# Two attention layers per image on one core: a loop of one pass with fixed score parts, a new order of a few steps, and x copied on chip

## What is computed

```
# layer 0
theta, phi = W_theta x + b_theta, W_phi x + b_phi        # 64 channels each
f   = softmax(theta^T phi / 8)                           # 1024 x 1024 per image
x1  = x + W_fuse (x f^T) + b_fuse
# layer 1
h   = group_norm(x1, 32 groups) * gn_w + gn_b
q, k, v = W_q h + b_q, W_k h + b_k, W_v h + b_v          # 128 channels
a   = softmax(q^T k / sqrt(128))                         # 1024 x 1024 per image
y   = x1 + W_p (v a^T) + b_p
```

## Time and profile before

| what | us |
|---|---|
| runs, median of 3 (lowest, highest) | 2093.81 (2093.53, 2098.11) |
| profiled execution, its own time | 2101.46 |
| span of its instructions | 2099.7 |
| PE / DVE / ACT / POOL busy in the span | 1800.1 / 1626.3 / 1522.8 / 1549.4 |
| share of the DMA engines' time used by the kernel's queue | 73.8% |
| HBM read / written | 67.64 MB / 17.04 MB |

### The profile page before, as it was taken

One profiled execution on the slowest core, in us unless ns is written; L12 is line 12 of the kernel. 1 busy time (PEld: TensorE's weight loads), 2 busy tenths in 40 slices (PEclk: granted clock), 3 DMA queues, 4 the chain that ended last, 5 costly groups with the idle time before them and its releaser, 6 DMA issues.

```text
span 2099.7 us, 32489 instructions
## 1 busy us (share of the span) xinstructions
PE 1800.1 (86%) x8388; PEld 1417.1 (67%) x8388; DVE 1626.3 (77%) x1706; ACT 1522.8 (73%) x2249; POOL 1549.4 (74%) x1605
## 2 busy tenths in 40 slices
PE   5788888888888888888888888888888888888886
PEld 4567676666676667667666766666776667677765
DVE  5687887787888688777877887887788788878864
ACT  5577777777777677677767776776777677777754
POOL 3577777777777777777767777777777677787764
PEclk8899999999999999999999999999999999999999
DMA  5578777777777777777777777787777677777774
GB/s 116 101 145 159 142 155 149 154 140 151 149 153 157 135 148 155 149 144 146 145 146 149 149 162 142 139 157 149 145 150 148 138 146 156 157 151 153 146 127 90
DMA packets 864787, 304.16 MB, mean 145 GB/s; under 512 B 822816, under 2 KB 823712, under 8 KB 864672
## 3 DMA queue, kind: packets, MB, share of 16 engines
q1 hardware_dynamic: 864672, 302.86, 73.8%
HBM read 67.64 MB, written 17.04 MB: 40 GB/s over the span
## 4 chain that ended last, share of the span: by engine, by line
PE 34%; issue 22%; ACT 17%; DVE 16%; POOL 4%; SPq 3%; DMA 2%; DVEq 1%; ACTq 0%; POOLq 0%
PE o_ps L365 11%; PE s_ps L365 9%; ACT s_ps L553 5%; PE s_ps L400 5%; PE m_ps L365 4%; DVE x L668 3%; ACT pair L576 3%; SPq L288 3%; PE m_ps L452 3%; DVE pair L636 2%; ACT et L564 2%; DMA pair_t<-pair 2%; DVE x L680 2%; DVE neg_max L619 2%; ACT e L553 2%
## 5 line engine op out<-in xcount | busy, mean ns | idle before, releaser
L744 POOL TENSOR_SCALAR et<-pair_t 128x2048 fp32r<-128x2048 f16 x384 | 747.5, 1950 | 168.4 <-DMA pair_t<-pair 165.4
L365 PE MATMUL o_ps<-et,v_hi 128*128 128x512 f32 x2048 | 755.9, 411 | 16.8 <-DVE y_sb L668 11.2
L619 DVE TENSOR_REDUCE neg_max<-s_ps 128x1 f32<-128x1024 f32 x512 | 622.0, 1215 | 114.7 <-PE s_ps L365 109.1
L636 DVE SCALAR_TENSOR_TENSOR pair<-s_ps,pair 128x1024 f16<-128x1024 f32 x384 | 467.5, 1218 | 28.8 <-ACT pair L576 28.4
L365 PEld LDWEIGHTS o_ps<-et,v_hi 128*128 128x128 f32 x2048 | 392.3, 192 | 107.4 <-issue 22.5
L553 ACT ACTIVATE s_ps<-s_ps,neg_max 128x1024 f32<-128x1024 f32 x384 | 418.1, 1089 | 22.5 <-DVE neg_max L619 16.3
L576 ACT ACTIVATE pair<-s_ps 128x1024 f16<-128x1024 f32 x384 | 392.9, 1023 | 20.9
L365 PE MATMUL o_ps<-et,v_lo 128*128 128x512 f32 x1024 | 407.5, 398 | 0.0
L630 DVE SCALAR_TENSOR_TENSOR et<-s_ps,et 128x1024 fp32r<-128x1024 f32 x128 | 156.8, 1225 | 262.8 <-ACT et L564 262.8
L365 PE MATMUL s_ps<-phi,theta 128*128 128x512 f32 x1024 | 289.7, 407 | 18.8 <-issue 13.5
L808 POOL TENSOR_TENSOR stage<-stage 128x256 f32<-128x256 f32 x256 | 188.2, 735 | 113.0 <-ACT stage L513 102.2
(11 more groups left out here) (88 smaller groups left out, 2484.7 us busy)
## 6 DMA issues: line engine op xcount, KB each, us to landing
rden_row<-rden_dram SPq DMA_DIRECT2D x128, 256.0 KB, 4.3
xs<-in_x SPq DMA_DIRECT2D x32, 512.0 KB, 4.7
phi<-phi SPq DMA_DIRECT2D x64, 256.0 KB, 4.2
xr<-in_x SPq DMA_DIRECT2D x32, 512.0 KB, 5.3
out_y<-y_sb SPq DMA_DIRECT2D x64, 256.0 KB, 2.5
pair_t<-pair SPq DMA_TRANSPOSE x384, 4.4
rden_dram<-rden SPq DMA_DIRECT2D x128, 2.0 KB, 1.6
w_f<-in_w_fuse_t SPq DMA_DIRECT2D x1, 64.0 KB, 2.6
```

The lines of the kernel that those rows point to most:

```text
L365: mm = pe.matmul(out, lhs_t, rhs, start=start and n == 0, stop=stop and n == len(terms) - 1)
L619: nc.vector.tensor_reduce(neg_max[:, t % 4:t % 4 + 1], s_ps[:, ring(it, t), :], AX.X, ALU.max, negate=True).then_inc(s_max, 1)
L636: nc.vector.scalar_tensor_tensor(out=pair[:, r, 1, :], in0=s_ps[:, r, :], scalar=E_SCALE, in1=pair[:, r, 0, :], op0=ALU.mult, op1=ALU.subt ...
L744: return nc.gpsimd.tensor_scalar(*args)
```

## The change

The loop has one pass per round: passes 2 to 30 are looped (29 rounds), and 31 to 33 are written out. The part of `s_ps` is fixed by the slot (`PART`); the `pair` and `pair_t` buffers go by the tile's place in its group. PE does the unit ahead of the transposes. DVE's residual of the first half moves from slot 11 to 12, its statistics to 13; the second half's stay in slot 15, and all of them now come after `reciprocals`. The reciprocals are written to DRAM turned over (4 rows of 128), so that the row is in the order of the output's columns. `xr` is no longer loaded: ACT copies it from `xs` in slot 3, and `xs` is loaded in slot 4, after that copy.

```diff
-RING = 3
-TURNED = (3,)
+TURNED = 3
+PART = (0, 1, 2, 0, 1, 2, 0, 1, 2, 0, 1, 2, 0, 1, 0, 2)
+PARTS = 3
+PAIRS = 3
...
-XS_SLOT = 1
-XR_SLOT = 6
+XR_SLOT = 3
+XS_SLOT = 4
...
+    def xr_at(g):
+        i, s = divmod(g, SLOTS)
+        return int(s == XR_SLOT and 0 <= i < NB)
...
+    def part(s):
+        return PART[s % SLOTS]
+
+    def part_before(i, s):
+
+        g = SLOTS * i + s
+        return next((p for p in range(g - 1, -1, -1) if tile_at(p) and part(p) == part(g)), None)
+
+    def until_part_before(kind, it, s):
+
+        return value(lambda i: count(kind, 0, (part_before(i, s) or 0) + 1), it)
...
-    LOOPED = (NB - 3 - 2) // RING * RING
...
-        with eng.Fori(0, LOOPED // RING) as j:
-            for n in range(RING):
-                body(It(j * RING + (2 + n), 2 + n, j))
-        for i in range(2 + LOOPED, NB + 2):
+        with eng.Fori(0, NB - 3) as j:
+            body(It(j + 2, 2, j))
+        for i in range(NB - 1, NB + 2):
             body(It(i, i, 0))
...
-        rden_dram = nc.dram_tensor("rden_dram", (2, P, GROUP), F32).ap()
+        rden_dram = nc.dram_tensor("rden_dram", (2, GROUP, P), F32).ap()
...
-                sp.wait_ge(s_et, before(free_of(crossed_at), it, t + 1))
+                sp.wait_ge(s_et, before(crossed_at, it, t - GROUP + 1))
...
-                sp.dma_start(rden_dram[g], rden[:, g, :]).then_inc(s_rden_dram[g], 16)
+                sp.dma_start(rden_dram[g].rearrange("t q -> q t"), rden[:, g, :],
+                             allow_slow_non_contiguous=True).then_inc(s_rden_dram[g], 16)
...
-                             rden_dram[g].rearrange("q t -> (q t)").partition_broadcast(P)).then_inc(s_rden_row[g], 16)
+                             rden_dram[g].rearrange("t q -> (t q)").partition_broadcast(P)).then_inc(s_rden_row[g], 16)
...
+                    sp.wait_ge(s_xr, before(xr_at, it, XS_SLOT + 1))
+                    sp.sem_inc(s_carrier)
                     sp.dma_start(xs[:, :], batch(x, i + 1)).then_inc(s_xs, 16)
-                if s == XR_SLOT and here(out0_at, it, OUT_LAG):
-                    sp.wait_ge(s_x1, before(out0_at, it, OUT_LAG))
-                    sp.sem_inc(s_carrier)
-                    sp.dma_start(xr[:, :], batch(x, i)).then_inc(s_xr, 16)
...
-                    if here(free_of(crossed_at), it, s):
-                        pe.wait_ge(s_pair, before(free_of(crossed_at), it, s + 1))
-                    if here(free_of(turned_at), it, s):
-                        pe.wait_ge(s_tlo, before(free_of(turned_at), it, s + 1))
+                    last = part_before(it.like, s)
+                    if last is not None and crossed_at(last):
+                        pe.wait_ge(s_pair, until_part_before(crossed_at, it, s))
+                    if last is not None and turned_at(last):
+                        pe.wait_ge(s_tlo, until_part_before(turned_at, it, s))
...
                     scores(it, s, 0)
                     scores(it, s, 1)
+                    unit(it, s)
                     transposes(it, s)
-                    unit(it, s)
                     values(it, s)
...
+                if here(xr_at, it, s):
+                    act.wait_ge(s_xs, 16 * before(x_at, it, s))
+                    act.wait_ge(s_x1, before(out0_at, it, OUT_LAG))
+                    nc.scalar.activation(xr[:, :], xs[:, :], ACT.Copy).then_inc(s_xr, 1)
...
-                nc.vector.tensor_tensor(to[:, cols].rearrange("c (t q) -> c t q", t=GROUP),
-                                        o_ps[:, :].rearrange("c (t q) -> c t q", t=GROUP),
-                                        rden_row[:, g, :].rearrange("c (q t) -> c t q", t=GROUP),
-                                        ALU.mult).then_inc(s_taken, 1)
...
+                nc.vector.tensor_tensor(to[:, cols], o_ps[:, :], rden_row[:, g, :], ALU.mult).then_inc(s_taken, 1)
...
-                    outputs(it, s)
-                    statistics(it, s)
+
+                    outputs(it, s - 1, 0)
+                    statistics(it, s - 2, 0)
+                    outputs(it, s, 1)
+                    statistics(it, s, 1)
```

More of the change, by code:

```diff
@@ L72, in crossed_at @@
     def crossed_at(g):
-        return int(tile_at(g) and g % GROUP not in TURNED)
+        return int(tile_at(g) and g % GROUP != TURNED)
     def turned_at(g):
-        return int(tile_at(g) and g % GROUP in TURNED)
+        return int(tile_at(g) and g % GROUP == TURNED)
     def unit_at(g):
@@ L110, in count, with value, same_pair @@
         return sum(what(g) for g in range(-SLOTS, SLOTS * i + s))
+    def value(at, it):
+        now = at(it.like)
+        if isinstance(it.i, int):
+            return now
+        return it.round * (at(it.like + 1) - now) + now
     def before(what, it, s):
[L114 to L117, removed]
+        return value(lambda i: count(what, i, s), it)
     def here(what, it, s):
         return bool(what(SLOTS * it.like + s))
[L122 to L136, removed]
+    def part(s):
[5 more added lines that the diff above has]
+        return value(lambda i: count(kind, 0, (part_before(i, s) or 0) + 1), it)
+    def same_pair(s):
+        return lambda g: int(crossed_at(g) and g % GROUP == s % GROUP)
     def same_group(s):
@@ L227, in attention_pair @@
         s_pair = sem("pair_ready")
-        s_pair_t = [sem(f"pair_transposed{n}") for n in range(RING)]
+        s_pair_t = [sem(f"pair_transposed{n}") for n in range(PAIRS)]
         s_tr = sem("transposed")
@@ L382, in scores @@
                         pe.wait_ge(s_direct, before(direct_at, it, 9))
-                out = s_ps[:, ring(it, s), half * HALF:(half + 1) * HALF]
+                out = s_ps[:, part(s), half * HALF:(half + 1) * HALF]
                 t = s % PHASE
@@ L546, in exponentials @@
                     return
-                n, r, g = before(tile_at, it, t), ring(it, t), t // GROUP % 2
+                n, r, g = before(tile_at, it, t), part(t), t // GROUP % 2
                 act.wait_ge(s_max, n + 1)
@@ L683, in statistics, with outputs @@
-            def statistics(it, s):
-                if not here(out0_at, it, s):
-                    return
-                half = (s - OUT_LAG) // GROUP % 2
+                nc.vector.tensor_tensor(to[:, cols], o_ps[:, :], rden_row[:, g, :], ALU.mult).then_inc(s_taken, 1)
+            def outputs(it, s, half):
+                cols = slice(half * HALF, (half + 1) * HALF)
+                if not (here(out0_at, it, s) and (s - OUT_LAG) // GROUP % 2 == half):
+                    return
+                dve.wait_ge(s_taken, before(group_at, it, s - OUT_LAG) + 1)
+                dve.wait_ge(s_xr, before(xr_at, it, s))
+                nc.vector.scalar_tensor_tensor(out=x1[:, cols], in0=x1[:, cols], scalar=vec[:, B_FUSE:B_FUSE + 1],
+                                               in1=xr[:, cols], op0=ALU.add, op1=ALU.add).then_inc(s_x1, 1)
@@ L687, in statistics @@
+            def statistics(it, s, half):
+                cols = slice(half * HALF, (half + 1) * HALF)
+                if not (here(out0_at, it, s) and (s - OUT_LAG) // GROUP % 2 == half):
+                    return
                 n = before(out0_at, it, s)
                 dve.wait_ge(s_x1, n + 1)
-                nc.vector.bn_stats(stats[:, half, :], x1[:, half * HALF:(half + 1) * HALF]).then_inc(s_stats, 1)
+                nc.vector.bn_stats(stats[:, half, :], x1[:, cols]).then_inc(s_stats, 1)
```

40 lines of the change are left out of this document (16 added, 24 removed).

## The result

The changed kernel takes **2478.36 us** (median of 4; 2476.01 to 2480.51) against 2095.96 for the kernel before on the same chip: 1.181 times as long (95% interval 1.179 to 1.184). Forecast: 2077, range 2043 to 2110. It is 382 us slower.

The account below looks back on a forecast made before the run. No engine was full; waits between engines bound each 16-slot pass (regular period 62.1 us). Loop -31.7, regular period 0 and clock +15.3 gave -16.4 from 2101.46; less 7.65 for the runs' median, 2077 us, range 2043 to 2110.

Parts of the forecast that it names:

- Product with the reciprocals in order: DVE's product in slots 7 and 15: -0.36 and -0.33 us per pass; the 512-piece write to DRAM costs nothing.
- Product in order: Reading the row in order makes DVE's product 0.32 us faster, saving 0.36 in slot 7 and 0.33 in slot 15.
- Rival 4: The product in order is no faster: 0.67 x 31 = +21 us on the forecast, 2098; chance 0.05.
- Fixed parts: Scores of slots 14 and 0 wait longer for DVE's rest: 1.26 us taken back in slot 14, +1.03 in slot 0.
- Order: Transposes behind PE's unit: -0.2 us in slot 8 and -0.26 in slot 9 per pass; slot 4 counted separately.
- k0's copy: Slot 4: the order moves this copy out of ACT's way, -1.03 us, set against the x copy's +0.95.
- Spread: First half's residual and statistics leave slot 11: PE reaches slot 13 1.08 us sooner; with slot 14's wait, +0.18.
- x copy: ACT's copy in slot 3 adds 0.95 us ahead of the exponential; against -1.03 in slot 4, net -0.08 per pass.
- The clock: Slot 0's PE idle grows to 2.4 us: 12 falls to half clock for 3, at 1.7 us each, +15.3 us.
- The loop: Single-pass loop: 28 jumps back at 0.28 us replace 8 at 4.9, so 39.5 go, 7.8 return: -31.7 us.
- Rival 3: Every jump back stalls as now, 28 x 4.9 us for 39.5: +113 with the clock, 2207 us; chance 0.05.

Follow-up runs that it names:

- e3: The changed kernel with the reciprocal row's load two slots later on SP: 2137.85 us, 1.0195 of the kernel before.
- e4: The changed kernel with the earlier reciprocal write and a straight product read (wrong column order, for time alone): 2056.10 us, 0.980 of the kernel before.
- e6: The changed kernel with the row assembled in SBUF by four DMAs, then written to DRAM as one piece: 2060.15 us, 0.982 of the kernel before.
- e7: The kernel before plus three edits only: transposes behind the unit, first half spread out, x copied on chip: 2021.29 us, 0.963.
- e10: e7 with the reciprocals by way of SBUF as in e6: 1981.88 us, 0.944 of the kernel before.
- e12: e6 with a loop body of three passes instead of one: 2060.50 us, 0.981 of the kernel before.
- f1: e7 with PE's transposes ahead of the unit again: 2061.50 us, 0.981 of the kernel before.
- f2: e7 with the first half's residual and statistics back in slot 11: 2101.22 us, 0.999 of the kernel before.
- f3: e7 with xr loaded by DMA in slot 6 and xs in slot 1, as before: 2019.65 us, 0.961 of the kernel before.
- e9: e1 with the second half's product left in PSUM, where the residual reads it: 2075.47 us, 0.988 of the kernel before.
- e1: The changed kernel with the reciprocals' write and product as before: 2164.84 us, 1.0305 of the kernel before.
- e5: e1 with the product walked query by query, PSUM operand and output in steps of 128: 2161.19 us, 1.0307 of the kernel before.
- e8: e1 with a loop body of three passes instead of one: 2129.74 us, 1.0162 of the kernel before.

## Why the prediction was wrong

**The step that failed** is the last of "Product with the reciprocals in order": "Between that write and the row's load SP takes 3.8 to 5.6 us anyway, and the row is used over 5 us later, so it costs nothing; without that cover DVE would wait at the product." It has two faults. It took the cover of before (5.6 us) as enough without bounding the landing of 512 pieces; this was 10.1 us. And it asked who uses the row (DVE, which waits for the row once at either product, 4.8 and 16.3 us) and not what is queued behind the wait, which is every transposition. Of the 382 us, 340 are SP's standing (the changed kernel against e3), 82 what the write's hold on the transpositions costs without it (e3 against e4), and the rest of the change gives 40 back (e4 against before). No rival of the five had this mechanism; the range missed by 368 us.

**What was left of the forecast**, read in e4 and e6, where the write costs nothing: 2056 and 2060 against 2077.

- *Product in order.* 0.32 taken, 0.38 measured. Rival 4 is out. With the row made by way of SBUF it gives 40 us in all (e7 against e10), for 0.69 x 31 = 21 in the sum; 0.06 more for each of two products makes 4 of the difference. By the passes, one without a fall goes from 59.9 to 59.0, 26 us, and 16 stretches at half clock become 11.
- *Fixed parts.* Slot 14 at 4.0 us after slot 13: 4.06, behind a wait of 0.68 (0.8 to 1.3 expected). PE idle in slot 0: 2.77 for 2.4. Price of all fixed parts by e12 against e10: 78.6 us, for 2.29 x 31 = 71 in the sum (1.03 for slot 0, 1.26 for slot 14). Right, though by the passes it is 2.0 in one without a fall (59.0 to 61.0) and the rest the clock, with 19 stretches at half clock for 11.
- *Order.* 40 us measured (f1) for 46 in the sum: 0.46 per pass, and the 1.03 of k0's copy, which the order also frees. Right in size, but only next to the spread: without it the order gives nothing (f2), which the sum did not have.
- *Spread.* 80 us measured (f2) for 1.08 per pass, 33 us. The direction was right and the size too small by more than half. 1.7 per pass (61.6 to 59.9) make 53, and 19 fewer stretches at half clock most of the rest; the sum had no term of the clock for this edit.
- *x copy.* 0.95 per pass taken against k0's copy, 29 us; measured 0. Without the copy, slots 4 and 5 take 3.88 and 4.84 us in place of 4.72 and 4.01 (medians of the passes): unit k1 waits for k_lo in either case, 0.73 us of idle PE with the copy and 1.32 without it in one pass of e7 and f3. The wait of 1.32 in the earlier trace rows was the row that said so, and I did not set the copy against it.
- *The clock.* 12 falls in 31 passes forecast. In e4, the change without the write's price, 18 of 31 passes have one and take 63.1 for 61.5; in e9 14 do, 63.85 for 62.4. The mechanism and the size (1.7 taken, 1.5 measured) were right, the number too low by half in e4. Its pass without a fall, 61.5, is 0.9 under the forecast 62.4 (62.1 and the jump's 0.28); e9's 62.4 does not bear that out, since its product still reads in steps. The changed kernel is worse off: one to four half-clock stretches in each pass, 92 in the run for 18 before. POOL's waits hand idle time on to PE; which idle led to which fall I did not follow up.
- *The loop.* -31.7 taken, 0 measured (e12 against e6), as above. The stalls are real and the short loop has none: the changed kernel fetches 8 + 14 instruction packets in its whole run (the earlier trace rows has 71 on one queue). Rival 3 is out. The Trainium skill (Runtime: NRT & Kernel Launch, Instruction fetch mechanics) says that a jump to a target outside a two-page window fetches it; as the prediction applied this to PE's pass, the trace does not agree, with 22 packets for 28 jumps and none of the stalls. Whether the rule or the size taken for the window is off, no run here shows. But I gave slot 0 a new idle of 2.4 us in the very place of the jump, without asking what of the stall it would have hidden.
- *Not seen at all:* the collision of residual and cast, 89 us in e1. In e1, with the product of before, the change moves slot 15's residual onto POOL's cast; the faster product pulls it out again, so in the changed kernel itself only 3 of 32 take over 1.5 us. The kernel before had the mild form in slot 11 (residual 0.91 for 0.75), and I took the 0.91 without asking why.

So the single terms cancel to a fair forecast of the rest (2077 for 2056), by luck in part: loop and x copy were each wrong by some 30 us in opposite directions, spread and product were too small, and the falls of the clock too few. The edits' single worths don't add up to the whole either, as f1 and f2 show.

**What stays open:** what makes the 512 pieces slow on the way to DRAM, and by what mechanism the write slows the packets of transpositions beside it. That it does is shown (6.3 us to land behind a write, 4.4 otherwise, in e3); the median of all, 4.5, hides it. The cause of either is not shown.

## What to carry to other kernels

When a DMA's shape changes, ask two things apart: how long it takes to land, with a bound from both sides, and what stands behind the wait for it on the issuing queue. The consumer may be well covered and the queue not. If an element order must be turned over, turn it on the way into SBUF and write whole rows to DRAM. And measure the parts of a change singly and next to each other: here order and spread gain 76 us together, and the order nothing without the spread; the x copy and the loop are worth nothing, the fixed parts cost 79, and the turned write costs 418 against the way through SBUF (e6). Only the sum was on the first page.

## What the runs showed of the hardware that was not expected

- 512 pieces of 4 bytes in one DMA to DRAM: 10.1 us from issue to landing. In four DMAs to SBUF, on the same queue: 2.0 each, 3.9 from the first issue to the last landing (e6). 128 pieces of 16 bytes to DRAM take 1.6.
- A transposition of 512 KB issued within 9.3 us behind such a write lands in 6.3 us, otherwise in 4.4 (medians, e3).
- A DVE instruction with two SBUF inputs that starts 0.01 us behind a POOL cast of 1.90 us takes 2.43 for 0.75; with one input in PSUM it takes 0.75 (e9). If it starts 0.36 us ahead of the cast, the two take 0.95 and 2.34 (e4).
- A float32 product of 128x512 takes 682 ns in order, 1063 ns with a step of four elements in the SBUF row, and 1063 to 1096 ns with a step of 128 elements in the PSUM operand and the output (e5).
- A loop whose body is one pass runs 28 jumps with 22 instruction packets in the whole run and 0.3 us of issue on DVE at each. With a body of three passes ACT's exponential shows issue time at 8 of 8 jumps in e7, e10, e12, f2 and f3, 29.1 to 39.7 us in total, and at 2 or 3 in f1 and e8.
